# Attention in one step loop: weighted sums behind both score pairs of the next tile, row maxima laid out by chunk

## What is computed

```
ql = x @ Wqd
q  = heads(ql @ Wqu)                 # 16 wide
qr = rope(heads(ql @ Wqr))           # 64 wide
ckv = x @ Wkvd
k, v = heads(ckv @ Wku), heads(ckv @ Wvu)
kr = rope(x @ Wkr)                   # 64 wide, one for all heads
scores = (q @ k.T + qr @ kr.T) / sqrt(16 + 64)
scores = where(causal, scores, -inf)
x = x + (softmax(scores) @ v) @ Wo   # x: (1, 2048, 256)
```

## Time and profile before

| | |
|---|---|
| median of three runs | 2878.74 us |
| the profiled execution | 2882.55 us |
| its span, first to last instruction | 2880.8 us |
| TensorE busy, share of the span | 2463.8 us, 86% |
| VectorE | 1714.8 us, 60% |
| ScalarE | 1346.1 us, 47% |
| GpSimd | 1088.1 us, 38% |
| mean granted clock of TensorE | 0.946 |

### The profile page before, as it was taken

How to read it: one execution, slowest core, us unless ns; L and a number is a source line. 1 busy time by engine, 2 the same in 40 slices (tenths; PEclk the granted TensorE clock), 3 DMA queues, 4 the chain that set the end, 5 groups by cost and what they waited for, 6 DMA issues and landing times. The chain is left out here.

```text
span 2880.8 us, 44554 instructions
## 1 busy us (share of the span) xinstructions
PE 2463.8 (86%) x15815; PEld 1887.0 (66%) x15815; DVE 1714.8 (60%) x3579; ACT 1346.1 (47%) x2718; POOL 1088.1 (38%) x989
## 2 busy tenths in 40 slices
PE   4967888988988986796979989888968998898798
PEld 4855545544544544685867777677758887776687
DVE  7556754755745734655454997979835544545443
ACT  3424345344444444342226886768644444433232
POOL 2642101101102101452223663636446666757232
PEclk9987999999999996898989999999979999999899
DMA  4242000000000003223010000000033233323200
GB/s 160 80 123 67 16 9 15 19 16 9 18 9 14 5 1 108 69 82 109 30 38 8 1 1 8 1 8 1 8 110 89 83 90 94 98 83 99 88 1 30
DMA packets 77332, 136.58 MB, mean 47 GB/s; under 512 B 25792, under 2 KB 47256, under 8 KB 75968
## 3 DMA queue, kind: packets, MB, share of 16 engines
q0 software_dynamic: 26336, 73.01, 8.5%
q1 hardware_dynamic: 50784, 60.72, 6.6%
HBM read 112.48 MB, written 20.81 MB: 46 GB/s over the span
## 5 line engine op out<-in xcount | busy, mean ns | idle before, releaser
L1442 ACT ACTIVATE PT<-ps 128x512 f32<-128x512 f32 (+3 forms) x640 | 302.9, 535 | 416.4 <-PE ps L1199 415.9
L2304 POOL DMA_INDIRECT KV<-kv_scratch,sidx x384 | 369.2, 962 | 213.9 <-issue 132.8
L35 PE MATMUL ps<-KIh,qih 128*128 128x512 f32 (+2 forms) x640 | 247.8, 387 | 50.5 <-DVE Isc L1888 40.8
L1319 DVE TENSOR_REDUCE xn<-ps 128x1 f32<-128x512 f32 x384 | 238.2, 682 | 70.7 <-PE ps L1184 70.7
L1948 POOL TENSOR_TENSOR part_sum<-part_sum,rlp 128x1024 f32<-128x1024 f32 (+7 forms) x120 | 210.6, 1755 | 86.6 <-ACT rlp L1774 85.4
L36 PE MATMUL ps<-KIl,qih 128*128 128x512 f32 (+2 forms) x640 | 239.4, 374 | 0.0
L1888 DVE SCALAR_TENSOR_TENSOR Isc<-ps,iw,Isc 128x1024 f32<-128x1024 f32 (+7 forms) x216 | 208.6, 966 | 51.7 <-ACT ps L1798 46.1
L37 PE MATMUL ps<-KIh,qil 128*128 128x512 f32 (+2 forms) x640 | 238.5, 373 | 0.0
L1798 ACT ACTIVATE ps<-ps,iwa 128x1024 f32<-128x1024 f32 (+7 forms) x240 | 198.2, 858 | 47.3 <-PE ps L37 46.6
L2226 ACT ACTIVATE sP<-sP,snm 128x128 f32<-128x128 f32 (+2 forms) x256 | 110.4, 432 | 232.5 <-DVE snm L2289 229.4
L35 PEld LDWEIGHTS ps<-KIh,qih 128*128 128x128 f32 x640 | 123.6, 193 | 96.0 <-issue 74.6
(11 more groups left out here) (356 smaller groups left out, 6763.1 us busy)
## 6 DMA issues: line engine op xcount, KB each, us to landing
cs<-in_rope SPq DMA_DIRECT2D x20, 512.0 KB, 4.1
ycomb<-y_rows SPq DMA_DIRECT2D x16, 512.0 KB, 4.9
w1raw<-in_w SPq DMA_DIRECT2D x14, 512.0 KB, 6.7
KV<-kv_scratch,sidx POOLq DMA_INDIRECT x384
xn_rows<-xnr SPq DMA_DIRECT2D x8, 512.0 KB, 4.9
w2raw<-in_w SPq DMA_DIRECT2D x14, 256.0 KB, 7.0
wir<-in_wi SPq DMA_DIRECT2D x1, 2176.0 KB, 7.8
X<-in_x SPq DMA_DIRECT2D x1, 2048.0 KB, 8.3
```

The costliest lines, as they stand in the source:

```text
L35: pe.matmul(out, lhs[0], rhs[0], start=start, stop=False)
L1319: v.tensor_reduce(mp[:, row, s:s + 1], o, AX_X, ALU.max).then_inc(a_free, 1)
L1442: s.activation(PT[:, rnd % 2, hh, lo:CH], ps[:, BANK[kind, u, j, r, hh % 2], lo:CH], ACT.Exp, scale=SCALE).then_inc(a_exp, 1)
L2304: g.indirect_dma_start(KV[:, BG * (k % RB) + m, :], None, a["kv_scratch"], bass.IndirectOffsetOnAxis(sidx[:, t % 2, at:at + 1], 0)).then_i ...
```

## The change

Two edits in the functions that make the list, and what follows from them. In `attend` the second score pair of tile `j` is yielded ahead of the weighted sum of tile `j - 1`, and no longer behind it. In `prepare` an M step is one chunk of one row of its own, through the new helper `maxima`, and `blend` places each by itself. The helper yields the chunks before the diagonal one by one and then the diagonal one. The cost that `blend` counts for a row stays nearly the same (0.47 (c + 1) + 0.08 before, 0.49 (c + 1) now, in us). The numbering of the banks and the waits follow the new steps.

```diff
+        def maxima(c):
+
+            yield from ((s,) for s in range(c))
+            yield (c,)
...
-                order += [("M", u, p, r) for r in range(CT)]
+                order += [("M", u, p, (r, chunks)) for r in range(CT) for chunks in maxima(u % NCH)]
...
                 yield "S", u, j, 0
+                yield "S", u, j, 1
                 if j >= 1:
                     yield "A", u, j - 1, 0
                 elif u >= 1:
                     yield "A", u - 1, CT * ((u - 1) % NCH + 1) - 1, 0
-                yield "S", u, j, 1
...
             if step[0] == "M":
-                return 0.47 * (step[1] % NCH + 1) + 0.08
+                return 0.47 * len(step[3][1]) + 0.02
...
-            for k_ in range({"K": 2, "P": 3, "M": 2 * (u_ % NCH + 1), "R": 1, "F": 1, "G": 2, "S": 2}.get(kind_, 0)):
+            for k_ in range({"K": 2, "P": 3, "M": 2 * len(r_[1]) if kind_ == "M" else 0, "R": 1, "F": 1, "G": 2, "S": 2}.get(kind_, 0)):
...
-                    for s in range(c + 1):
-                        wide = CH if s < c else max(2 * P, (r + 1) * P)
+                    for at, s in enumerate(chunks):
+                        wide = CH if s < c else max(2 * P, (row + 1) * P)
                         keys = slice(CH * s, CH * s + wide)
-                        o = [take(kind, u, p, r, 2 * s + k) for k in range(2)]
+                        o = [take(kind, u, p, r, 2 * at + k) for k in range(2)]
...
-                    v.wait_ge(a_free, PIECE["M", u, NP - 1, CT - 1, 2 * c + 1] + 1)
+                    v.wait_ge(a_free, PIECE["M", u, NP - 1, (CT - 1, (c,)), 1] + 1)
```

More of the change, by code:

```diff
@@ L1171, in attn_tensor @@
                 elif kind == "M":
-                    p, tok = h, slice(r * P, (r + 1) * P)
+                    p, (row, chunks) = h, r
+                    tok = slice(row * P, (row + 1) * P)
                     pe.wait_ge(a_qhi, NP * u + p + 1)
@@ L1313, in attn_vector @@
                 elif kind == "M":
-                    for s in range(c + 1):
-                        for k in range(2):
-                            o = full(kind, u, h, r, 2 * s + k)
-                            row = CT * (NP * k + h) + r
-                            if s < c:
-                                v.tensor_reduce(mp[:, row, s:s + 1], o, AX_X, ALU.max).then_inc(a_free, 1)
-                            else:
-                                end = (r + 1) * P
-                                seen = cm_bf[:].rearrange("p a t -> p (a t)")[:, CH - end:CH]
-                                v.tensor_tensor_reduce(out=o[:, 0:end], in0=o[:, 0:end], in1=seen, scale=1.0, scalar=LEAST,
-                                                       op0=ALU.add, op1=ALU.max, accum_out=mp[:, row, s:s + 1]).then_inc(a_free, 1)
+                    at, (s,) = r
+                    for k in range(2):
+                        o = full(kind, u, h, r, k)
+                        part = mp[:, CT * (NP * k + h) + at, s:s + 1]
+                        if s < c:
+                            v.tensor_reduce(part, o, AX_X, ALU.max).then_inc(a_free, 1)
+                        else:
+                            end = (at + 1) * P
+                            seen = cm_bf[:].rearrange("p a t -> p (a t)")[:, CH - end:CH]
+                            v.tensor_tensor_reduce(out=o[:, 0:end], in0=o[:, 0:end], in1=seen, scale=1.0, scalar=LEAST,
+                                                   op0=ALU.add, op1=ALU.max, accum_out=part).then_inc(a_free, 1)
                 elif kind == "X":
-                    v.wait_ge(a_free, PIECE["M", u, NP - 1, CT - 1, 2 * c + 1] + 1)
+                    v.wait_ge(a_free, PIECE["M", u, NP - 1, (CT - 1, (c,)), 1] + 1)
                     if u >= 1:
```

## The result

The changed kernel takes 2805.98 us (median of four runs, 2802.44 to 2811.05), the kernel before on the same chip 2877.56 us (four runs, 2873.49 to 2880.06). The ratio is 0.9754, with a 95% interval of 0.9732 to 0.9776: 71.6 us less. The profiled execution took 2802.95 us, its span is 2801.2 us, against 2882.55 and 2880.8 before.

A forecast was written before the change was run, and what follows sets the result against it. TensorE was taken as first in all units, with VectorE close in the 4-, 8- and 12-tile ones. Terms 13.8 + 7.3 + 28.0 + 4.0 + 11.0 = 64.1 us gave 2815 us, range 2797 to 2854.

The forecast's parts named there:

- Swap, 16-tile units: Second score pair ahead of the weighted sum removes waits in three 16-tile units that prepare another: 4.6 us each, 13.8.
- Last unit: In the last 16-tile unit, with nothing to prepare, waits before sums go except the very last one: 7.3 us.
- Split, 12-tile unit: In four 12-tile units maxima by chunk cut VectorE's dry time: stretch 43.2 us for 50.2, 28.0 in all.
- moves as a whole: Chain behind the 12-tile unit's maxima (transpose, negation, DMA, next scores) stays unchanged and swallows the diagonal sums' gains: nothing counted.
- 8-tile unit: In four 8-tile units VectorE already sets the pace; half of its 2.1 us dry time goes: 4.0 us.
- 4-tile unit: First maxima start 1.5 us sooner, VectorE's 1.95 dry is covered: 3.0 in three units, 2.0 in the first, 11.0.
- Clock: Rival: TensorE's clock swings, all four kinds of unit run at 0.94, 50 us come back: 2865; chance 0.04.
- Ring: Rival: two pairs in a row hold four of seven banks, TensorE stands for exponentials: 100 us lost, 2915; chance 0.07.
- VectorE's pace: Rival: VectorE's unchanged work on maxima sets the pace, the split gives nothing: 25.6 us gained, 2853; chance 0.20.

The follow-up runs named there:

- early split: The change with the step that splits the second head pair's queries moved ahead of the first pair's last row of maxima: 2977.32 us, ratio 0.9749.
- longer lead: The change with the planner ending the next unit's preparation 8 us ahead of its use, not 5: 3001.73 us, ratio 0.9819 to the kernel before.
- a1_six_banks: The change with a ring of six PSUM banks for the step loop, not seven: 2988.58 us, ratio 0.9862 to the kernel before.

## Why the prediction was right, and where its terms were off

The time, 2805.98, stands 9 us below the forecast of 2815 and inside the range; the case is the forecast's and no rival's. The sum was 6.5 us too small in the loop (70.6 for 64.1), with terms off both ways.

- **Swap, 16-tile units: right, mis-sized.** 5.6 us each where 4.6 was said. The round without a wait is 3.06 us, as worked out. The swap alone gives 6.0 (69.9 to 63.9) and the new waits for banks take 0.4 of it back, where 0.8 was charged. So the gain in front of that charge was 6.0 and not 5.4; part of the stands was booked as work.
- **Last unit: right.** 8.3 where 7.3 was said. The sum that stays waits 0.71 us and not 1.28 (the other pair now runs in front of the sum ahead of it); the rest of the 1.0 us is of the same kind as above.
- **Split, 12-tile unit: the mechanism right, one step wrong.** VectorE's dry time was put at 3.3 and is 3.2 to 3.7 us. From the copy of sums to the column of maxima the forecast was 4.4 + 43.2 = 47.6 us, the 43.2 with the later start in it; measured are 5.0 us to the first maximum and 43.3 from there, 48.3. VectorE is busy for 39.55 us in the window and not 38.96. A part of that 0.6 is that a run of reductions that is broken up takes longer: in the last row six full maxima took 2.48 and 1.29 us (four, then two), where six in a run take 3.68. TensorE's demand was put at about 39 us and is 40.5, by the run with halved maxima. The step that failed is that the chain behind "moves as a whole" and "swallows whatever the diagonal sums would have gained by themselves". It went from 8.5 to 6.7 us. TensorE there, before, after, and with the split alone (timelines):

```profile
1039.54 0.85 PE L1212 MATMUL ps<-PT,VG 128*32 128x384 f32 x8 [1.24 <-ACT PT L1442]
...
1040.98 0.28 PE L1188 MATMUL ps<-ident,xn 128*16 128x128 f32 x1
```
```profile
974.99 0.85 PE L1218 MATMUL ps<-PT,VG 128*32 128x384 f32 x8
976.50 0.27 PE L1194 MATMUL ps<-ident,xn 128*16 128x128 f32 x1 [0.65 <-DVE xn L1335]
```
```profile
1002.65 0.85 PE L1218 MATMUL ps<-PT,VG 128*32 128x384 f32 x8
...
1004.10 0.28 PE L1194 MATMUL ps<-ident,xn 128*16 128x128 f32 x1
```

  The column of maxima was begun by VectorE at 1039.31, but its transpose stood on TensorE behind a diagonal sum that waited 1.24 us for exponentials, and came at 1040.98, 1.67 later. Now that sum doesn't wait, and the transpose starts 0.37 us after the column (976.13 to 976.50), waiting for nothing but it. That is 1.3 us earlier. Either edit by itself does most of it: with the split alone that sum doesn't wait either, and the transpose starts 0.45 us after its column (1003.65 to 1004.10); with the swap alone 0.91 after it. From the negation to the first scores it is 2.85 us in both (1041.30 to 1044.15, 976.80 to 979.66): TensorE stands there longer, 1.19 for 0.30, because it is done sooner, and the chain is no shorter. The other 0.55 us lie between these scores and the copy of the sums (3.70 and 3.15 us), and they are the swap's: the split alone still has 3.70. So a unit gained 8.1 us, not 7.0: 1.8 more behind the maxima, 0.7 less up to them.
- **8-tile unit: near in size, in three of four units by luck.** 0.7 to 0.8 us in three units, 3.5 in the first, 5.8 for 4.0. The prediction let the split halve VectorE's dry time. Alone it does more than that (2.0 to 0.8 us dry, 1.8 us gained), and the swap puts it back to 2.0, where it was. What the three units gain comes from elsewhere: 0.5 us because the first maximum comes earlier, the rest in small pieces. In the first of the four the dry time does fall, from 3.7 to 1.1 us. That the two edits act against each other here was not in the working.
- **4-tile unit: too high.** 1.1, 3.6 and 3.3 us in three units (3.0 was said), and the first, for which 2.0 was said, lost 0.6. The spread is the clock's: the unit that gained least, 29.6 to 28.5, holds a half-clock stretch only after, the two others only before. At full clock in both the unit goes from 29.6 to 27.0, so 2.6. The first maxima came earlier for the reason given, the copy's wait no longer in front of them: 0.9 us from the copy to the first maximum, for 2.5. It is the swap that does it: the swap alone has the same 27.0. The 1.95 us for which VectorE is dry in the earlier trace rows were read in a unit with the half-clock stretch; in the unit of 29.6 us they are 1.28.
- **Clock.** The granted clock is 1.00 in all five units shown, where the earlier trace rows have 0.94 in one and 0.99 in one. Over the whole loop it is 0.99, as before, so the rival fell:

```profile
275.00:1029.00 754.00, 709.41 (x5535) 419.58 (x5534) 475.14 (x1093) 370.63 (x773) 116.62 (x123) 0.99 0.05 13
```

  What a half-clock stretch costs was told wrong, though. The prediction put nothing for it, because the unit waits for VectorE anyway; the kernel before has the same unit once without it, 29.6 us at clock 1.00 for 30.3 at 0.94. In the change one lies in the second group's 4-tile unit (windows):

```profile
494.00:496.00 2.00, 2.00 (x19) 0.96 (x17) 0.00 (x0) 1.40 (x5) 0.44 (x1) 0.50 0.02 4
```

  TensorE is busy throughout and VectorE not at all, so here TensorE sets the time, and the unit is 28.5 us for 27.0. It can also cost nothing, as in the early split, and there is more of it in the kernel with six banks and in the one with the longer lead. 4-tile units of these, in this order, two of each of the first two kernels (windows):

```profile
669.90:696.70 26.80, 22.97 (x165) 13.65 (x167) 22.27 (x59) 9.20 (x23) 5.77 (x7) 0.94 0.08 22
858.80:885.60 26.80, 22.01 (x165) 12.41 (x167) 22.24 (x59) 9.20 (x23) 5.80 (x7) 1.00 0.07 21
...
682.50:710.50 28.00, 21.72 (x165) 12.49 (x167) 22.30 (x59) 9.14 (x23) 5.78 (x7) 1.00 0.08 21
880.00:909.20 29.20, 25.35 (x165) 14.03 (x167) 22.47 (x59) 9.05 (x23) 5.80 (x7) 0.82 0.07 20
...
877.70:908.90 31.20, 25.93 (x169) 15.27 (x171) 22.39 (x59) 9.27 (x23) 5.83 (x7) 0.84 0.07 19
```

  By the Trainium skill (TensorE: Matmul & The Clock Gate, "A second HAM failure mode: psum-queue depth-cycling") cycling through banks with short stands can make the clock swing. The trace of the change doesn't bear that out: it has 65 short stands for maxima over the loop (lines 1188 and 1205 among its waits), and its clock is no lower than before. But with six banks, where these stands are more (95), two of three 4-tile units run at 0.82 and 0.83, and with the longer lead all three at 0.84. Against the stands as the whole cause speaks that units of one kernel with the same work in the same order are at 1.00 and at 0.82. What makes the clock fall in one and not in the other stays open.
- **Ring.** 0.8 us of waits for exponentials in three places, where 0.67 us a tile was the point from which it decides. a1_six_banks shows a different danger that the rivals did not have: with one bank fewer a third of the gain goes, mostly by waits for maxima.
- **VectorE's pace.** As a rival it fell, but more was in it than the 0.20 says. After the change VectorE's work still sets much of the pace of the 4-, 8- and 12-tile units: halving its full reductions takes 3.7, 3.9 and 2.6 us from them. In the 12-tile unit it shares it with TensorE (39.6 and 40.5 us of work in a stretch of 43.2). What the rival missed is that VectorE's work could set the pace and the split still give 7 us, since its dry time was inside the pace.

What stays open: why VectorE was dry longer in the first group's 8-tile unit before, which gained 3.5 us and the others 0.8; what lets the clock fall in some 4-tile and 12-tile units; how much of the split's gain is the overrun of the ring at VectorE's full work; and how much of the 32 us by which PE's busy time fell are stands booked as work.

## What to carry to other kernels

Where two engines are nearly level, cost a reordering by the dry time of the slower one between its first and last instruction of a unit, and then look at what the consumer's own queue holds in front of the step that ends the chain: in this kernel the first came out to 0.7 us of 47.6, and a transpose queued behind a waiting sum was the miss. Lay a producer's bursts so that the consumer is never dry, and test each of two orderings alone in each kind of unit: here one gave nearly everything in the long units and the other most in the 12-tile ones, and in the 8-tile unit they cost each other 1 us. A gap that remains is found by the same row: 2.13 us of VectorE's idle time was worth 1.4 us when one step was moved.

## What the runs showed of the hardware that was not expected

- One PSUM bank fewer, of seven, costs 23.8 us of 822 from norm to last copy though only 2.8 us are waits for exponentials; in the last unit, without maxima, it costs nothing. Some of it is time at half clock.
- Semaphore waits that are met already, two or three for each chunk of a row, cost nothing that was measured: 2987.17 and 2987.23 us with and without most of them.
- A matmul that waits costs more than its idle time says: the swap took 6.0 us from a 16-tile unit in which the trace books 3.9 for exponentials and 0.8 for the copy.
- Chips differ by 5 to 6% in this kernel before (2877.56; 3032.43, 3053.46 and 3047.75), and not in the attention: the change has the same units to 0.1 us on two of them.
- TensorE's clock can be at half for 3.4 us of a 26.8 us unit at no cost, and for 10 us in one of two units with the same work (0.82 and 1.00): units have to be compared by their clock as well.
